# An adaptive-norm transformer layer on one core: the join of attention and MLP, its loads, its projection and its weight splits

## The chip, the cores and the metric

The kernel runs on one core of a Trainium2 chip. The metric is the device time of one execution in microseconds; lower is better. TensorE (PE) multiplies, VectorE (DVE), ScalarE (ACT) and GpSimd (POOL) work on tiles, SyncE (SP) issues most DMAs. Each engine runs its own list of instructions in order and waits on semaphores for the others.

## The reference, cut

```python
mod = (silu(c) @ wmod).reshape(8, 6, 1, 512)
sa, ca, ga, sb, cb, gb = (mod[:, i] for i in range(6))
ga, gb = ((2 * (g >= 0) - 1) * maximum(abs(g), 0.25) for g in (ga, gb))
h = layernorm(x) * (1 + ca) + sa                 # x: 8 x 512 x 512
x = x + ga * attention(h, W_attn, W_proj)        # 16 heads of 32, causal
h = layernorm(x) * (1 + cb) + sb
x = x + gb * (relu(relu(h @ W1.T + b1) @ W2.T + b2) @ W3.T + b3)   # 512-1024-1024-512
```

## The kernel before

Each fp32 product is made of three products of a high and a low part: a `hi` step rounds a tile to the matmul's format on ScalarE, a `lo` step subtracts it from the whole value on VectorE, and TensorE multiplies hi*hi, hi*lo and lo*hi (`TERMS`). A tile of weights therefore needs a `_hi` and a `_lo` step before its first use.

**Attention** runs batch by batch, 0 to 7. A batch has eight slots p (pairs of heads), a slot has five units u. In unit (p, u) TensorE makes scores by query of pair p, scores by key of pair p - 2, in units 1 and 3 the weighted values of pair p - 3 (10 matmuls of each of two kinds), and pieces of the QKV projection. VectorE takes row maxima from the scores (two score banks), splits the maxima into `max_rows` in unit 2, and two DMAs of 4 KB carry them into `stack`, where the key scores of pair p - 1 need them in the next slot. ScalarE exponentiates key scores twice (`prob_hi`, `prob`), GpSimd (four units) and VectorE (one) make `prob_lo`. The last batch goes on to slot 11, with no projections of a next batch; its scores end in slot 7, its key scores in slot 9, its weighted values in slot 10.

**The join.** In the slots of that batch every engine calls a function `early(p, u)` at the end of each unit, which begins the second half of the layer in that engine's list; `rest()` follows when the slots are over. What is to be done for the first batch k = 0 (and partly k = 1): load `at` (attention output), `wproj`, `xt` (`res_tiles`), the gate `ga` and four blocks of W1; turn `at` with transposes (`TURNED`, four times four) through two `aux` banks and split it (`turned_hi`, `turned_lo`); project it, four tiles of 12 matmuls (`PROJ`); gate, add the residual and take statistics (`rows(t)` on VectorE); the inverse deviation on GpSimd; normalise on ScalarE; turn again (`ROWS`), modulate into `h2`. Tiles of this half lie on SBUF that attention has used, so a load waits until its place is free: the methods of `Released` wait on attention's semaphores for that.

**The MLP** is a Strassen-like scheme of seven products per layer and batch: n = 0 to 7 are the chunks of the first layer (`expand`), 8 to 15 of the second, 16 to 23 of the third. Operand s of chunk n is made by sums on VectorE, `hi(n, s)` and `lo(n, s)`; the W1 side needs four sums (`w1_sum`) and seven splits (`w1_hi`, `w1_lo`). Between the products of chunk k stand the aux pieces of later batches (`AUX_AT`): PROJ(k+1, 2) and (k+1, 3) after products 0 and 1, TURNED(k+2) in 2 and 3, ROWS(k+1) in 5 and 6.

The names `w_0` to `w_6` in the lists below are the seven splits of W1 (`w_s_whole` is the whole value), `lin` and `aux` are PSUM banks, `op` is an MLP operand, `gated`, `res_tiles` and `bn_stats` belong to `rows(t)`.

## Time and profile before

| | us |
|---|---|
| median of three runs | 1503.06 (1500.37 to 1503.61) |
| the profiled execution | 1500.26 |
| its span, first to last instruction | 1498.5 |
| PE busy in the span | 1432.5 (96%) |
| DVE busy | 1111.7 (74%) |
| ACT busy | 811.2 (54%) |
| POOL busy | 447.9 (30%) |

### The profile page before, as it was taken

The page shows a single profiled execution, that of the slowest core. Times are in us where ns is not written, and L with a number is a line of the kernel's source. Part 1 is how long each engine was busy: PE and PEld are TensorE (multiplying, and loading weights), DVE is VectorE, ACT ScalarE, POOL GpSimd, SP SyncE. Part 2 cuts the span into 40 slices and gives each one's busy share as a digit, 9 for nine tenths or more (in the row PEclk, how much of TensorE's full clock was granted, in tenths as well). Part 3 has the DMA queues.
Part 4 walks back from the last instruction along what each step waited for, and adds up shares of the span by engine and source line. Part 5 has one row for each costly group of instructions (what it writes and reads, how often), then busy time and mean ns, then how long its engine had stood idle before and what let it go on. Part 6 is the DMA issues. An engine that isn't in the chain of part 4 may idle for free. (4 is left out here: it accounts for less than half of the span.)

```text
span 1498.5 us, 30337 instructions
## 1 busy us (share of the span) xinstructions
PE 1432.5 (96%) x12048; PEld 1284.9 (86%) x12048; DVE 1111.7 (74%) x1955; ACT 811.2 (54%) x1468; POOL 447.9 (30%) x450
## 2 busy tenths in 40 slices
PE   7999999999999999988699999999999999999998
PEld 4578787887878878876599999999999999999998
DVE  4687777777877777668676666797766676788887
ACT  3366666667676767666555555566333333354331
POOL 2375765666576667655200000000000000000000
PEclk9999999999999999999799999999999999999999
DMA  8625354443534343473344444644756556589985
GB/s 275 157 55 128 93 135 94 110 114 78 125 88 122 83 122 82 101 203 116 106 148 148 148 149 148 221 173 150 271 199 218 204 211 235 210 290 311 298 298 181
DMA packets 126589, 247.15 MB, mean 165 GB/s; under 512 B 13672, under 2 KB 36200, under 8 KB 126448
## 3 DMA queue, kind: packets, MB, share of 16 engines
q1 hardware_dynamic: 122416, 241.56, 51.6%
q10 hardware_dynamic: 4032, 3.66, 0.8%
q8 instruction: 95, 1.56, 0.4%
q14 instruction: 46, 0.38, 0.1%
HBM read 114.58 MB, written 79.72 MB: 130 GB/s over the span
## 5 line engine op out<-in xcount | busy, mean ns | idle before, releaser
L537 POOL TENSOR_TENSOR prob_lo<-prob,prob_hi 128x512 f16<-128x512 f32 x256 | 300.6, 1178 | 162.1 <-ACT prob L670 161.7
L663 ACT ACTIVATE prob_hi<-key_score 128x512 f16<-128x512 f32 x320 | 191.1, 597 | 150.8 <-PE key_score L1000 149.3
L2399 PE MATMUL sum_b<-op,w 128*128 128x256 f32 x1728 | 217.9, 284 | 3.4 <-DVE p_c L1957 1.7
L887 PE MATMUL lin<-h_parts,wqkv 128*128 128x512 f32 x768 | 215.1, 403 | 3.7 <-POOL h_parts L497 2.8
L2399 PEld LDWEIGHTS sum_b<-op,w 128*128 128x128 f32 x1728 | 211.3, 192 | 5.7 <-issue 3.7
L845 DVE TENSOR_REDUCE row_max<-score 128x1 f32<-128x512 f32 (+2 forms) x384 | 180.3, 498 | 22.1 <-PE score L987 21.3
L670 ACT ACTIVATE prob<-key_score 128x512 f32<-128x512 f32 x320 | 190.6, 596 | 0.0
L887 PEld LDWEIGHTS lin<-h_parts,wqkv 128*128 128x128 f32 x768 | 139.4, 191 | 33.5 <-DVE h_parts L718 5.4
L987 PE MATMUL score<-stack 96*128 96x512 f32 (+3 forms) x512 | 154.7, 363 | 0.0
L2399 PE MATMUL sum_e<-op,w 128*128 128x256 f32 x1152 | 146.7, 284 | 2.3 <-issue 1.4
L1000 PE MATMUL key_score<-stack 98*128 98x512 f32 (+3 forms) x512 | 143.8, 343 | 4.7 <-DMA stack<-max_rows 4.7
L2399 PE MATMUL sum_a<-op,w 128*128 128x256 f32 x1152 | 145.5, 284 | 0.9 <-issue 0.9
L2399 PEld LDWEIGHTS sum_e<-op,w 128*128 128x128 f32 x1152 | 141.7, 192 | 3.2 <-issue 1.6
L2399 PEld LDWEIGHTS sum_a<-op,w 128*128 128x128 f32 x1152 | 141.2, 192 | 1.8 <-issue 1.0
L1020 PEld LDWEIGHTS o_bank<-v_parts,prob_hi 128*128 128x128 f16 x1280 | 98.4, 98 | 23.5 <-issue 20.8
L1020 PE MATMUL o_bank<-v_parts,prob_hi 128*128 128x97 bf16 x1280 | 115.0, 210 | 0.9 <-issue 0.9
L1020 PE MATMUL o_bank<-v_parts,prob_lo 128*128 128x65 bf16 x1280 | 112.0, 194 | 0.0
L897 PE MATMUL lin<-wqkv,h_parts 128*128 128x256 f32 x768 | 108.8, 284 | 0.0
L897 PEld LDWEIGHTS lin<-wqkv,h_parts 128*128 128x128 f32 x768 | 102.1, 190 | 5.0
L1020 PEld LDWEIGHTS o_bank<-v_parts,prob_lo 128*128 128x128 f16 x1280 | 99.8, 99 | 0.2
L2332 PE MATMUL aux<-wproj,turned 128*128 128x512 f32 x384 | 94.7, 399 | 2.8 <-DVE gated L1824 1.5
L1000 PEld LDWEIGHTS key_score<-stack 98*128 98x128 f32 x512 | 83.9, 193 | 6.1 <-DMA stack<-max_rows 6.0
(164 smaller groups left out, 2555.7 us busy)
## 6 DMA issues: line engine op xcount, KB each, us to landing
stack<-qk_parts SPq DMA_DIRECT2D x384, 128.0 KB, 2.4
late_op_whole<-y_dram SPq DMA_DIRECT2D x40, 512.0 KB, 5.3
y_dram<-u_c SPq DMA_DIRECT2D x32, 512.0 KB, 3.4
blk<-y_dram SPq DMA_DIRECT2D x32, 512.0 KB, 4.2
y_dram<-y_sum SPq DMA_DIRECT2D x24, 512.0 KB, 3.5
x_tiles<-x SPq DMA_DIRECT2D x32, 256.0 KB, 3.7
attn_dram<-o_rows SPq DMA_DIRECT2D x32, 256.0 KB, 2.3
attn_tiles<-attn_dram SPq DMA_DIRECT2D x8, 1024.0 KB, 6.1
```

What stands on the lines that cost most here:

```text
L537: nc.gpsimd.tensor_tensor(prob_lo[:, key[1] % 2, u, :], prob[:, u, :], prob_hi[:, key[1] % 2, u, :], ALU.subtract).then_inc(lo_pool, 1)
L663: nc.scalar.activation(prob_hi[:, q % 2, u, :], bank[:], ACT.Exp, scale=SOFTMAX_SCALE, bias=P_SHIFT)
L670: nc.scalar.activation(prob[:, u, :], bank[:], ACT.Exp, scale=SOFTMAX_SCALE, bias=P_SHIFT)\
L845: last = nc.vector.reduce_max(row_max[:, p % 2, hh, t:t + 1], bank[:, col:col + P * (t + 1)], AX.X)
L887: mm = nc.tensor.matmul(lin_bank_of((QK, f))[:], wqkv[:, wl, c, at:at + P], h[:, hl, c, :], start=(c == 0 and k == 0), stop=(c == NC_ - 1 ...
L897: mm = nc.tensor.matmul(lin_bank_of((V, g, t))[:, 0:C // 2], h[:, hl, c, t * P:(t + 1) * P], wqkv[:, wl, c, at:at + C // 2], start=(c == 0 ...
L987: mm = nc.tensor.matmul(bank[:, col:col + n], rows[:, 0, t * P:(t + 1) * P], rows[:, 1, 0:n], start=False, stop=True, skip_group_check=True)
L1000: mm = nc.tensor.matmul(bank[:, col:col + n], rows[:, 1, t * P:(t + 1) * P], rows[:, 0, t * P:T], start=False, stop=True, skip_group_check ...
L1020: mm = nc.tensor.matmul(o_bank[:, i * VW + low:(i + 1) * VW], part[:, p % 2, u, at:at + P], v[:, j, head, low:VW], start=(j == 0 and part ...
L2332: mm = nc.tensor.matmul(bank[:], turned[:, dl, c, t * P:(t + 1) * P], wproj[:, wl, c, :], start=(c == 0 and i == 0), stop=(c == NC_ - 1 an ...
L2399: mm = nc.tensor.matmul(dst, w[:, wl, c, cols], data[:, dl, c, :], start=begin, stop=end, skip_group_check=again)
```

## The change

- **SBUF.** The QKV weights become two tensors, `wqk` and `wv`; the tensors of the second half are placed in another order, so that `wproj`, `norm_tiles` and `attn_tiles` lie where the query and key weights were. Those weights are last read in unit (3, 1), the value weights in slot 4.
- **SyncE.** The loads for k = 0 and 1 are 256 KB each (W1's too, so `w1_in` counts 32), one a unit, and each unit from slot 3 on first waits for that unit's last score (`unit_reached`). `wproj` is issued at (3, 2) to (4, 0), `at` of batch 0 in slot 4, `xt` in slot 5; before, they were issued at (4, 3) and (5, 0).
- **TensorE.** TURNED of batch 0 moves from slot 6 to units (5, 2) to (6, 0). Its projection, four times 12 matmuls in slots 7 and 8, becomes sixteen times 3, one a unit from (6, 0) and two in (8, 4). The ROWS transposes stand together at (10, 4).
- **ScalarE and VectorE.** The splits of `wproj` and `turned` move with them. `rows(t)` moves to (6, 4), (7, 3), (8, 2), (9, 0); the last sum of W1 to (10, 0), the inverse deviation (GpSimd) to (9, 1). The splits of W1: before, 1 to 6 in a row after operand 0; now split 1 at (10, 4), ahead of operand 0 on VectorE, and 2 to 6 between the steps of the first chunk.
- **ScalarE in every expand chunk:** `hi(n, 6)` ahead of `relu(n, C11)`, not behind it.

```diff
         def early(p, u):
-            if (p, u) == (NEXT_FROM, 3):
+            if p >= 3:
+                released.unit_reached(sp, p, u)
+            if (p, u) == (3, 2):
+                released.query_key_weights(sp)
+            if p == 3 and u >= 2:
+                load_proj(u - 2)
+            if (p, u) == (4, 0):
+                load_proj(3)
+            if p == 4 and u:
+                load_at_tile(0, u - 1)
+            if (p, u) == (5, 0):
                 released.projections(sp)
-                released.projections_taken(sp)
-                load_at(0)
-                sp.dma_start(wproj_whole[:, 1], wproj_t.rearrange("(c p) n -> p c n", p=P)).then_inc(proj_in, 16)
...
+        def unit_reached(self, engine, p, u):
+            if p < PAIRS:
+                engine.wait_ge(score_done, unit_no(B - 1, p, u) + 1)
+            elif p < PAIRS + 2:
+                engine.wait_ge(key_done, unit_no(B - 1, p - 2, u) + 1)
...
         def early(p, u):
-            if p == 6 and u in (1, 2):
-                proj_lo(u - 1)
-            if p == 6 and u:
-                turned_lo(0, u - 1)
-            if p == 7 and u < 2:
-                w1_sum(u)
-            if p in (7, 8) and u in (2, 4):
-                rows(2 * (p - 7) + u // 2 - 1)
+            if (p, u) == (4, 4):
+                proj_lo(0)
+            if (p, u) == (5, 1):
+                proj_lo(1)
+            if p == 5 and u >= 2:
+                turned_lo(0, u - 2)
+            if (p, u) == (6, 0):
+                turned_lo(0, 3)
+            if (p, u) in ((6, 4), (7, 3), (8, 2), (9, 0)):
+                rows(((6, 4), (7, 3), (8, 2), (9, 0)).index((p, u)))
+            if (p, u) == (7, 1):
+                w1_sum(0)
             if (p, u) == (8, 0):
+                w1_sum(1)
+            if (p, u) == (8, 3):
                 w1_sum(2)
-            if (p, u) == (8, 4):
+            if (p, u) == (9, 0):
                 variance(0)
...
+            if (p, u) == (10, 0):
                 w1_sum(3)
...
+            if (p, u) == (10, 4):
+                w1_lo(1)
...
+        def project_part(k, t, c):
+            bank = aux_bank[AUX_NO[(PROJ, k, t)] % 2]
+            if k == 0 and t == 0 and c % 2 == 0:
+                pe.wait_ge(w_ready, W_NO[("proj", c // 2)] + 1)
+            if t == 0:
+                pe.wait_ge(att_lo, NC_ * k + c + 1)
+            if c == 0:
+                aux_free((PROJ, k, t))
...
         def early(p, u):
-            if p == 6 and u < NC_:
-                aux((TURNED, 0, u))
-            if p in (7, 8) and u in (0, 2):
-                aux((PROJ, 0, 2 * (p - 7) + u // 2))
+            if p == 5 and u >= 2:
+                aux((TURNED, 0, u - 2))
+            if (p, u) == (6, 0):
+                aux((TURNED, 0, 3))
+            if p in (6, 7, 8):
+                part = UNITS * (p - 6) + u
+                project_part(0, part // NC_, part % NC_)
+            if (p, u) == (8, 4):
+                project_part(0, 3, 3)
...
+            hi(n, 6)
             relu(n, C11)
-            hi(n, 6)
```

The three `early` functions above are SyncE's, VectorE's and TensorE's; the last three lines are ScalarE's `expand`.

SyncE's list at the end of attention, from the store of a group of output rows on, before:

```order
L447 DMA attn_dram<-o_rows 128x4x128
L1311 DMA attn_tiles<-attn_dram 128x4x512
L1393 DMA wproj_whole<-wproj_t 128x4x512
L1317 DMA res_tiles<-x 128x4x512
L1322 DMA gate_attn<-gate_dram 128x512 x2
L447 DMA attn_dram<-o_rows 128x4x128
L453 DMA stack<-max_rows 1x8x128 x2
L1401 DMA w_0_whole<-w_t 128x2x512
L1402 DMA w_2_whole<-w_t 128x2x512
```

and now:

```order
L464 DMA attn_dram<-o_rows 128x4x128
L1426 DMA wproj_whole<-wproj_t 128x512 x4
L1420 DMA attn_tiles<-attn_dram 128x512 x4
L1423 DMA res_tiles<-x 128x512
L464 DMA attn_dram<-o_rows 128x4x128
L1423 DMA res_tiles<-x 128x512
L470 DMA stack<-max_rows 1x8x128 x2
L1423 DMA res_tiles<-x 128x512 x2
L1349 DMA gate_attn<-gate_dram 128x512
L1433 DMA w_0_whole<-w_t 128x512 x2
L470 DMA stack<-max_rows 1x8x128 x2
```

The loads have become single tiles, `wproj` comes first, and the maxima (`stack<-max_rows`) have tiles of `res_tiles` and W1 between them instead of whole blocks.

TensorE's list around the start of the projection, at units (7, 0) and (7, 1) before:

```order
L969 MATMUL score<-mask_qk,ident_bf 128x128
L974 MATMUL key_score<-mask_kq,ident_bf 128x128
L987 MATMUL score<-stack 128x512
L1000 MATMUL key_score<-stack 128x512
L2332 MATMUL aux<-wproj,turned 128x512 x12
L969 MATMUL score<-mask_qk,ident_bf 128x256
L974 MATMUL key_score<-mask_kq,ident_bf 128x256
L987 MATMUL score<-stack 128x384
L987 MATMUL score<-stack 128x128
L1000 MATMUL key_score<-stack 128x128
L1000 MATMUL key_score<-stack 128x384
```

and at (6, 0) and (6, 1) now (the last transposes of `attn_tiles` ahead of the first quarter):

```order
L1004 MATMUL score<-stack 128x512
L1017 MATMUL key_score<-stack 128x512
L2404 MATMUL aux<-ident,attn_tiles 128x128 x4
L2416 MATMUL aux<-wproj,turned 128x512 x3
L986 MATMUL score<-mask_qk,ident_bf 128x256
L991 MATMUL key_score<-mask_kq,ident_bf 128x256
L1004 MATMUL score<-stack 128x384
L1004 MATMUL score<-stack 128x128
L1017 MATMUL key_score<-stack 128x128
L1017 MATMUL key_score<-stack 128x384
```

Twelve projection matmuls behind one unit have become three behind each, and they begin a slot earlier.

VectorE's list from the last gather of attention to the first gate of the first chunk, before:

```order
L809 TENSOR_REDUCE o_sum<-o_bank 128x4x32
L812 RECIPROCAL o_rcp<-o_bank 128x4
L1859 TENSOR_TENSOR op_sum<-h 128x512
L1917 TENSOR_TENSOR op<-h,op 128x512
L1981 TENSOR_TENSOR w_1<-w_1_whole,w_1 128x1024
L1981 TENSOR_TENSOR w_2<-w_2_whole,w_2 128x1024
L1981 TENSOR_TENSOR w_3<-w_3_whole,w_3 128x1024
L1981 TENSOR_TENSOR w_4<-w_4_whole,w_4 128x1024
L1981 TENSOR_TENSOR w_5<-w_5_whole,w_5 128x1024
L1981 TENSOR_TENSOR w_6<-w_6_whole,w_6 128x1024
L1824 TENSOR_TENSOR gated<-aux,gate_attn 128x512
```

and now:

```order
L826 TENSOR_REDUCE o_sum<-o_bank 128x4x32
L829 RECIPROCAL o_rcp<-o_bank 128x4
L2050 TENSOR_TENSOR w_1<-w_1_whole,w_1 128x1024
L1928 TENSOR_TENSOR op_sum<-h 128x512
L1986 TENSOR_TENSOR op<-h,op 128x512
L1893 TENSOR_TENSOR gated<-aux,gate_attn 128x512
L1934 TENSOR_TENSOR op_whole<-h,op_sum 128x512
L1941 TENSOR_TENSOR op_sum<-op_whole,h 128x512
```

Five of the six splits of W1 are gone from ahead of the gate; split 1 has moved ahead of the first operand's sum and split.

## Rows read from the trace of the kernel before

**Rows 1.** The page's slices, 37.5 us each: TensorE and its granted clock.
```profile
PE   7999999999999999988699999999999999999998
...
PEclk9999999999999999999799999999999999999999
```

**Rows 2.** Windows: us, busy (xcount) of PE, PEld, DVE, ACT, POOL, PEclk, DMA share, GB/s.
```profile
662.40:674.15 11.75, 8.14 (x68) 6.33 (x68) 5.75 (x15) 5.32 (x12) 5.43 (x6) 0.71 0.91 324
674.15:685.45 11.30, 7.62 (x84) 6.27 (x84) 9.80 (x20) 8.39 (x15) 7.47 (x6) 1.00 0.66 230
685.45:700.21 14.76, 13.43 (x94) 10.48 (x92) 10.81 (x21) 5.82 (x11) 5.38 (x5) 0.77 0.25 69
700.21:709.40 9.19, 9.12 (x81) 7.32 (x80) 8.44 (x18) 6.20 (x12) 6.48 (x5) 1.00 0.22 84
709.40:729.47 20.07, 8.04 (x69) 6.55 (x70) 12.27 (x21) 11.10 (x20) 10.44 (x9) 0.67 0.19 66
...
653.85:740.17 86.32, 65.38 (x562) 53.98 (x560) 58.13 (x114) 51.15 (x93) 42.65 (x38) 0.82 0.43 136
665.00:672.00 7.00, 5.49 (x35) 4.30 (x36) 2.65 (x7) 2.56 (x5) 2.84 (x3) 0.51 1.03 374
685.60:692.40 6.80, 5.47 (x15) 3.85 (x13) 4.27 (x6) 2.56 (x5) 3.87 (x3) 0.50 0.22 73
716.30:733.40 17.10, 8.73 (x66) 8.05 (x67) 6.27 (x13) 7.33 (x12) 3.86 (x4) 0.50 0.13 48
```

**Rows 3.** Timeline of TensorE: start, us, what, in brackets the wait ahead and its releaser.
```profile
666.51 0.80 PE L1000 MATMUL key_score<-stack 98*128 98x512 f32 x1 [3.54 <-DMA stack<-max_rows]
...
717.74 1.11 PE L2320 MATMUL aux<-ident,attn_tiles 128*128 128x128 f32 x4 [4.24 <-DVE turned L1814]
...
729.47 0.90 PE L2342 MATMUL aux<-ident,norm_tiles 128*128 128x128 f32 x3 [6.93 <-ACT norm_tiles L1588]
...
740.17 3.03 PE L2399 MATMUL sum_a<-op,w 128*128 128x256 f32 x24
...
744.70 3.06 PE L2332 MATMUL aux<-wproj,turned 128*128 128x512 f32 x12 [1.50 <-DVE gated L1824]
```

**Rows 4.** SyncE's timeline at slot 4's end, then the page's DMA issues (us to landing).
```profile
659.53 0.36 SPq L1311 DMA_DIRECT2D attn_tiles<-attn_dram  x1
...
x_tiles<-x SPq DMA_DIRECT2D x32, 256.0 KB, 3.7
...
attn_tiles<-attn_dram SPq DMA_DIRECT2D x8, 1024.0 KB, 6.1
```

**Rows 5.** VectorE's groups by form, 660 to 745 us, and GpSimd's timeline beside L1991.
```profile
L1814 DVE TENSOR_TENSOR turned<-aux,turned 128x512 fp32r<-128x512 f32 x8 | 5.5, 683 | 5.1 <-ACT turned L1580 5.1
...
L1976 DVE TENSOR_TENSOR wproj<-wproj_whole,wproj 128x1024 fp32r<-128x1024 f32 x2 | 2.7, 1354 | 0.4 <-ACT wproj L1657 0.4
...
L1991 DVE TENSOR_TENSOR w_whole<-w_whole,w_whole 128x1024 f32<-128x1024 f32 x1 | 2.1, 2071 | 0.0
...
L1995 DVE TENSOR_TENSOR w_whole<-w_whole,w_whole 128x1024 f32<-128x1024 f32 x1 | 1.2, 1216 | 0.0
...
688.28 1.16 POOL L537 TENSOR_TENSOR prob_lo<-prob,prob_hi 128x512 f16<-128x512 f32 x1 [0.31 <-ACT prob L670]
```

**Rows 6.** Timeline of VectorE.
```profile
697.63 0.67 DVE L1824 TENSOR_TENSOR gated<-aux,gate_attn 128x512 f32<-128x512 f32 x1
...
700.00 0.72 DVE L845 TENSOR_REDUCE row_max<-score 128x1 f32<-128x384 f32 x2
...
743.96 0.68 DVE L1824 TENSOR_TENSOR gated<-aux,gate_attn 128x512 f32<-128x512 f32 x1
...
761.02 0.68 DVE L1917 TENSOR_TENSOR op<-op_sum,op 128x512 fp32r<-128x512 f32 x1
```

**Rows 7.** Timeline of ScalarE ahead of the ROWS transposes.
```profile
726.49 2.93 ACT L1588 ACTIVATE norm_tiles<-res_tiles,mlp_shift,rstd 128x512 f32<-128x512 f32 x4 [2.35 <-DVE mlp_shift L1850]
```

**Rows 8.** Waits of TensorE from 747 to 1025 us: total, times, longest.
```profile
PE sum_b L2399 <- DVE p_c L1957: 1.7, 7, 0.3
```

More of the change, by code:

```diff
@@ L258, in w_block, with w_part @@
         return tile[:, :, W_ORDER[k]:W_ORDER[k] + W_BLOCK]
+    def w_part(part, k):
+        first = W_ORDER[k]
+        if first < 2 * C:
+            return wqk[:, part, :, first:first + W_BLOCK]
+        return wv[:, part, :, first - 2 * C:first - 2 * C + W_BLOCK]
     def w_ready(f):
@@ L1227, in mlp @@
     const_in, gb_in = mem.sem("const_in"), mem.sem("gb_in")
-    at_in, proj_in = mem.sem("at_in"), mem.sem("proj_in")
+    at_in = mem.sem("at_in")
+    proj_in = [mem.sem(f"proj_in{i}") for i in range(2)]
     w1_in = [mem.sem(f"w1_in{i}") for i in range(4)]
@@ new lines, in early @@
+        def early(p, u):
+            if p >= 3:
[9 more added lines that the diff above has]
+            if (p, u) == (5, 0):
+                released.projections(sp)
+            if p == 5 and u < NT:
+                load_x_tile(0, u)
+            if (p, u) == (5, 4):
@@ L1407, in early @@
-            if (p, u) == (6, 3):
-                load_x(1)
+            if (p, u) == (6, 0):
+                released.value_rest(sp)
+            if p == 6 and u < 4:
+                load_w1(u // 2, u % 2)
+            if (p, u) == (6, 4):
+                released.key_scores(sp, 3)
+            if (p, u) in ((6, 4), (7, 0)):
+                load_w1(2, p - 6)
+            if (p, u) in ((7, 1), (7, 2)):
+                load_w1(3, u - 1)
+            if (p, u) in ((7, 3), (7, 4), (8, 0), (8, 1)):
+                load_at_tile(1, 2 * (p - 7) + (u - 3 if p == 7 else u))
@@ L1653, in proj_hi @@
         def proj_hi(half):
-            if half == 0:
-                act.wait_ge(proj_in, 16)
+            act.wait_ge(proj_in[half], 32)
             c = 2 * half
@@ L1712, in rest @@
             released.probabilities(act)
-            for s in range(1, STEPS):
+            for s in (1, 2):
                 w1_hi(s)
@@ L1730, in expand @@
             first_product(n)
+            if n == 0:
+                w1_hi(3)
             hi(n, 3)
+            if n == 0:
+                w1_hi(4)
             hi(n, 4)
+            if n == 0:
+                w1_hi(5)
+                w1_hi(6)
             if last:
@@ L2127, in rest @@
             lo(0, 0)
-            for s in range(1, STEPS):
-                w1_lo(s)
             released.outputs(dve)
@@ L2156, in expand @@
                 add_rows(k + 1, 1)
+            if n == 0:
+                w1_lo(2)
             lo(n, 2)
+            if n == 0:
+                w1_lo(3)
             if k == B - 2:
@@ L2321, in turn_attention @@
             mm.then_inc(aux_done, 1)
-        def project(k, t):
-            bank = aux_bank[AUX_NO[(PROJ, k, t)] % 2]
-            if k == 0 and t == 0:
-                pe.wait_ge(w_ready, W_NO[("proj", 1)] + 1)
-            if t == 0:
-                pe.wait_ge(att_lo, NC_ * (k + 1))
-            aux_free((PROJ, k, t))
+        def project_part(k, t, c):
+            bank = aux_bank[AUX_NO[(PROJ, k, t)] % 2]
+            if k == 0 and t == 0 and c % 2 == 0:
+                pe.wait_ge(w_ready, W_NO[("proj", c // 2)] + 1)
+            if t == 0:
+                pe.wait_ge(att_lo, NC_ * k + c + 1)
+            if c == 0:
+                aux_free((PROJ, k, t))
+            for i, (wl, dl) in enumerate(TERMS):
+                mm = nc.tensor.matmul(bank[:], turned[:, dl, c, t * P:(t + 1) * P], wproj[:, wl, c, :],
+                                      start=(c == 0 and i == 0), stop=(c == NC_ - 1 and i == 2))
+            if c == NC_ - 1:
+                mm.then_inc(aux_done, 1)
+        def project(k, t):
             for c in range(NC_):
-                for i, (wl, dl) in enumerate(TERMS):
-                    mm = nc.tensor.matmul(bank[:], turned[:, dl, c, t * P:(t + 1) * P], wproj[:, wl, c, :],
-                                          start=(c == 0 and i == 0), stop=(c == NC_ - 1 and i == 2))
-            mm.then_inc(aux_done, 1)
+                project_part(k, t, c)
         def turn_rows(k, c):
@@ L2407, in early @@
         def early(p, u):
-            if p == 6 and u < NC_:
-                aux((TURNED, 0, u))
-            if p in (7, 8) and u in (0, 2):
-                aux((PROJ, 0, 2 * (p - 7) + u // 2))
+            if p == 5 and u >= 2:
+                aux((TURNED, 0, u - 2))
+            if (p, u) == (6, 0):
+                aux((TURNED, 0, 3))
[4 more added lines that the diff above has]
+                project_part(0, 3, 3)
             if p == 9 and u < NC_:
                 aux((TURNED, 1, u))
-            if p == 10 and u < NC_:
-                aux((ROWS, 0, u))
+            if (p, u) == (10, 4):
+                for c in range(NC_):
+                    aux((ROWS, 0, c))
             if p == 11 and u in (1, 3):
```

115 lines of the change are left out of this document (68 added, 47 removed).

## The prediction

> **What bounds the kernel now.** The page comes first: its slices show TensorE at nine tenths or more nearly everywhere except at the start and in slices 18 to 20, and the clock dips in one of those slices too [rows 1]. 37 us a slice puts the place at 640 to 750 us, where attention hands over to the MLP. Second come windows cut at the borders of the attention slots [rows 2]. From 653.85 us (last batch, slot 4) to 740.17 us (first MLP product [rows 3]) there are 86.3 us, of which TensorE is busy 65.4, so 20.9 us are idle. Three stretches stand at half clock (5.5, 5.5 and 8.7 us of busy time), so about half of 19.7 us, 9.8 us, is lost to the clock. At full clock and without a gap TensorE would need 55.6 us. Third comes the timeline of TensorE: it waits 3.54 us for two 4 KB rows of maxima (slot 5), 4.24 us for VectorE's split of turned attention (slot 9), 6.93 us for ScalarE's normalised rows before the ROWS transposes, 1.50 us for VectorE in the first products [rows 3]. The other engines say what would be next: VectorE is busy 58.1 us of the same 86.3 [rows 2], more than TensorE's 55.6 us of true work. Behind the join, TensorE has next to no waits (0.3 us in each of seven expand chunks [rows 8]), so what is gained before the first product reaches the end of the program one for one.
>
> **Slots 5 to 9, the base.** They run 11.75, 11.30, 14.76, 9.19 and 20.07 us, 67.1 us to the ROWS transposes at 729.47; slot 5 carries attention alone, 5.75 us of VectorE [rows 2]. Prices on VectorE: a quarter-megabyte split of wproj 1.35 us, half of turned 0.6 us (0.68 each, overlapped in sequence), sums of W1 2.07 us once and 1.2 us afterwards [rows 5], a group of gate, residual and statistics 697.63 to 700.00, 2.4 us [rows 6].
>
> **Loads one slot sooner.** Before, 3 MB are issued from 659.53 us on and the rows of maxima have to get through them [rows 4]; that is the 3.54 us wait. After it, wproj goes out in four portions behind the stack rows, some 3 us before that time, and the attention tiles one a unit from 658 us. I take 2 MB over some 8 us instead of 3 MB at once, and take the wait from 3.54 to 1 us; bounds 0 and 3.54. What is behind it on SP: the maxima of slots 5 to 8 stand in the same queue, each behind at most the portion of the unit before. Here the Trainium skill ("DMA: Bandwidth & Descriptors", Rules for kernel authors) speaks against the change: for bandwidth it wants 1 MiB or more in a DMA. The trace agrees in part: 256 KB land in 3.7 us and 1024 KB in 6.1 us [rows 4], so four portions one behind another would take 14.8 us where one took 6.1. By that rule the last attention tile, issued at about 662.5, would have to wait for its predecessors and land near 673 rather than 666, and the gain would be about 5 us smaller; the transfers of the profile overlap, so I keep to 3.7 us.
>
> **Slot 5.** VectorE now has 5.75 of attention, both wproj splits (2.7; the first falls at slot 4's end) and three turned splits (1.8): 10.3 us, and I add 1.4 us of hand-overs where it waits for ScalarE's high parts: 11.7 us. The slot is no shorter than before (11.75), but it carries work that before filled slot 6.
>
> **Slots 6 and 7.** TensorE: attention at full clock 5.3 us (slot 7's 14.76 less 1.3 idle, 2.7 clock and two projections of 2.7) and five quarters of 0.69: 8.8, with the last transpose 9.2. VectorE: 5.75 + 0.6 + 2.4 = 8.8 in slot 6; 5.75 + 2.07 + 2.4 = 10.2 in slot 7. The longer one counts: 9.3 and 10.2. Before it was 11.30 + 14.76.
>
> **Slot 8.** Keys alone. VectorE: gathers, maxima and one low part 2.3, two sums of W1 2.4, one group of rows 2.4: 7.1; TensorE six quarters 4.1 and attention 3.4: 7.5. With one hand-over (the turn of the maxima waits for slot 7's last maximum) 8.0.
>
> **Slot 9 up to ROWS.** The last group of rows 2.4, variance 0.2, four turned splits in step with TensorE and ScalarE, then the last probabilities of the pair, the normalisation 2.9 [rows 7]: 12.5 us. Before 20.07: there W1's fourth sum and first split stood ahead of the turned splits and the deviation stood behind the last low parts on GpSimd; after, it is asked for at (9, 1) and lies ready, and the sum and the split (1.2 + 1.2 to 2.2) lie in the shadow of ScalarE. The normalisation itself stays exposed.
>
> These five give 11.7 + 9.3 + 10.2 + 8.0 + 12.5 = 51.7 us against 67.1: **15.4 us** gained.
>
> **ROWS to the first product.** Before 740.17 - 729.47 = 10.7 us, four of them at half clock. After: four transposes paced by ScalarE's modulation 2.8 us, two projections of 2.8: 8.4 us, **2.3 us** gained. VectorE has a new wait here: W1's split 1 stands ahead of the first operand and needs ScalarE's copy, which stands behind modulation and the operand's copy. I put the operand at 7.6 us from the first ROWS transpose, so 0.8 us before TensorE wants it: it costs nothing; without that cover it would be up to 1.2 us.
>
> **First products.** Before, six splits in a row held up the gate of VectorE until 743.96, and TensorE waited 1.50 us [rows 3, 6]. After, that gate stands ahead of four of them: 1.5 us gained. Given back: five splits, 5.8 us, now stand between the sums of the first chunk. From 743.96 to the split of operand 5 at 761.02 VectorE does not pause [rows 6], 17.7 us with that split. It starts 0.8 us before the first product and so ends 17.7 + 5.8 - 0.8, or 22.7 us, behind it; TensorE wants operand 5 at 21.9. I charge 0.8 us, bounds 0 and 3. Net **0.7 us**.
>
> **Order on ScalarE in every expand chunk.** Copy 6 goes ahead of four relus. Before, the sum of C22 stood behind it and TensorE waited 0.3 us in seven chunks, 1.7 us in all [rows 8]. I take all of it: **1.8 us** with the first chunk. The relus move back by 0.5 us and nobody waits for them so closely.
>
> Of the other edits (split of the QKV tensor in two, places of tiles, 32 in place of 16 to wait for) nothing takes time of its own. The number of matmuls and of bytes stays.
>
> **Sum.** 15.4 + 2.3 + 0.7 + 1.8 = 20.2 us. Against it I set what such a sum doesn't see: TensorE still idles some 4 us of 12 in slots 5 and 9, and each of the two shorter dips of before began after idle time and cost 2.7 us. I take one (2.7) and 1.5 us for hand-overs between the engines: 4.2. The gain is **16 us**. The profiled execution took 1500.26 us (span 1498.5 and 1.8 around it), so 1484.3. The three runs have a median of 1503.06 and reach from 1500.37 to 1503.61, so the profiled one is at their lower end; I put the forecast at **1485**.
>
> Port of VectorE and GpSimd: the first sum of W1 takes 2.07 us with GpSimd at work beside it from 688.28 on, and the others 1.2 us [rows 5]. The Trainium skill ("SBUF — State Buffer", Who interferes with whom) says that a VectorE instruction with two SBUF inputs contends with a GpSimd instruction that reads SBUF. Both splits of wproj and a second and a third sum of W1 now lie in slots in which GpSimd works most. By that rule all of them could cost 2.1 rather than 1.2 to 1.35 us, and the gain would be up to 3 us smaller.
>
> **Rivals.**
> 1. VectorE is the wall. It has 45 us of work in slots 5 to 9 and I let it be busy 88% where it was busy 70% (47.1 of 67.1 [rows 2]). If it stays at 78%, the five slots take 58 us, 6 us more, and two dips instead of one cost 2.7: 1494. For: the pieces come in threes behind ScalarE's copies, and TensorE has only two banks of scores. Against: in slot 8 before, it was busy 8.44 of 9.19.
> 2. Nearly everything goes: no dip and no hand-overs beyond those in the slots, 1500.3 - 20.2 = 1480, and if slot 5 is not bound by VectorE 3 to 5 us less, 1476. For: slots with projection in them had no gaps before (slot 8, 9.12 of 9.19).
> 3. Slower: the maxima wait behind portions. The place is the first key score of slots 5 to 9. If the 4 KB rows meet a portion in flight in each and wait the measured 3.54 us, and each wait brings a dip of 2.7 us, it is five times 6.2, 31 us, less the one such wait and dip of before (6.2): 25 against the gain of 20.2, 1505. It turns at about 80% of that price in every slot. Against: the DMA engines were 0.91 busy over the whole of slot 5 [rows 2], and only that one wait came of it.
> 4. It doesn't do what it says: the portions come too late for (5, 2), each unit holding the next load back, and the order gains nothing in slots 5 and 6; the later parts stay: about 1497 to 1500.
>
> **How the numbers follow.** Forecast 0.55, rival 1 0.22, rival 2 0.13, rival 3 0.05, rival 4 0.05. The range 1476 to 1495 holds the first three with their bounds (nine in ten, and some lies beyond). A measurement here tells 0.2%, 3 us, from no change. Faster takes the first three and a part of rival 4, 0.92; same the rest of rival 4, 0.03; slower 0.05.
>
> **What would show it.** The wait of TensorE for the maxima at the first key score of slot 5 at 1 us or less; turned splits in slot 5; the first batch's projection in threes, nowhere twelve in a row; ROWS at about 714 and the first product at 722 to 725; no 1.5 us wait at the second projection of the first chunk, a wait of up to 1 us at operand 5; no wait at C22. Half clock in 10 us or less of the join instead of 31. Wrong, if VectorE's share in slots 5 to 9 is below 80% while TensorE waits for it, or if TensorE waits for maxima in more than one slot.

## The result and the profile after

The changed kernel took 1490.26 us (median of four runs, 1489.35 to 1492.82) beside 1502.53 us for the kernel before; ratio **0.9914, 95% interval 0.9897 to 0.9931**. Two later comparisons gave 0.9901 (0.9880 to 0.9922) and 0.9897 (0.9878 to 0.9916). The gain is 12 to 15 us; 1485 was forecast.

The profiled execution took 1489.35 us, span 1487.6, that is 10.9 us less than the span before. The page's slices of TensorE and its granted clock [rows 1 before]:

```profile
PE   8999999999999999999799999999999999999998
PEclk9999999999999999999999999999999999999999
```

The slices at 8, 8 and 6 in the middle have become 9, 9 and 7, and the clock's 7 is gone. Windows cut at the same borders as in [rows 2] (slots 5 to 9, the ROWS transposes up to the first product, the whole from slot 4 to the first product, and the two stretches of half clock in it):

```profile
667.99:677.78 9.79, 8.40 (x80) 7.20 (x81) 8.65 (x18) 8.34 (x16) 6.97 (x6) 0.83 0.68 216
677.78:688.42 10.64, 9.84 (x88) 7.34 (x86) 8.48 (x21) 6.65 (x14) 5.62 (x6) 1.00 0.60 176
688.42:697.62 9.20, 9.17 (x83) 6.86 (x83) 8.92 (x18) 5.41 (x12) 6.67 (x5) 1.00 0.51 147
697.62:706.34 8.72, 8.05 (x74) 5.88 (x74) 7.34 (x15) 6.74 (x13) 5.88 (x6) 1.00 0.47 150
706.34:722.51 16.17, 8.73 (x111) 7.46 (x110) 13.65 (x24) 10.08 (x18) 9.65 (x8) 0.86 0.45 147
722.51:731.73 9.22, 8.90 (x43) 7.10 (x41) 4.09 (x7) 5.49 (x7) 0.62 (x1) 0.88 0.72 235
659.44:731.73 72.29, 61.41 (x561) 49.20 (x560) 56.59 (x114) 49.40 (x90) 41.89 (x38) 0.93 0.60 182
670.00:673.00 3.00, 3.00 (x20) 2.40 (x21) 2.37 (x5) 2.78 (x6) 2.35 (x3) 0.52 0.96 343
717.80:725.20 7.40, 5.56 (x52) 4.79 (x52) 3.94 (x6) 3.15 (x5) 2.27 (x3) 0.54 0.19 70
```

From slot 4 to the first product it is 72.3 us in place of 86.3: TensorE idles 10.9 us and not 20.9, and two stretches at half clock, some 10 us, are left of 31. VectorE was busy 56.6 of the 72.3 us.

But the span shrank by 10.9 us only, while the join gave 14.0 and the part behind it 2.4. The rest went the other way **ahead** of the join: slot 4 of the last batch starts at 659.44 in place of 653.85 us, 5.6 us later, in a part whose order of work the change leaves alone. The timeline of TensorE, with the waits that are left:

```profile
669.98 0.69 PE L1017 MATMUL key_score<-stack 98*128 98x512 f32 x1 [1.39 <-DMA stack<-max_rows]
...
709.25 0.20 PE L1037 MATMUL o_bank<-v_parts,prob_hi 128*128 128x97 bf16 x1 [1.57 <-DVE o_rcp L829]
...
712.52 0.66 PE L2404 MATMUL aux<-ident,attn_tiles 128*128 128x128 f32 x4 [1.56 <-DVE turned L1883]
...
718.00 0.24 PE L1037 MATMUL o_bank<-v_parts,prob_hi 128*128 128x97 bf16 x1 [2.60 <-POOL prob_lo L554]
...
721.15 0.27 PE L1037 MATMUL o_bank<-v_parts,prob_hi 128*128 128x97 bf16 x1 [1.63 <-DVE o_rcp L829]
...
722.51 3.47 PE L2431 MATMUL aux<-ident,norm_tiles 128*128 128x128 f32 x16
...
731.73 3.04 PE L2488 MATMUL sum_a<-op,w 128*128 128x256 f32 x24
734.61 2.91 PE L2416 MATMUL aux<-wproj,turned 128*128 128x512 f32 x12
...
754.14 1.67 PE L2488 MATMUL sum_e<-op,w 128*128 128x256 f32 x12 [0.64 <-DVE w L2050]
```

Against [rows 3]: the wait for the maxima went from 3.54 to 1.39 us and that for the split of turned attention from 4.24 to 1.56; the 6.93 us are gone, and so is the 1.50 us at the second projection (734.61 carries no wait). New between slot 9's start and ROWS are 2.60 us for GpSimd's low part and 1.57 and 1.63 us for VectorE's gatherings, and behind the first product 0.64 us at operand 5. SyncE's timeline, to set beside [rows 4]:

```profile
662.68 0.54 SPq L464 DMA_DIRECT2D attn_dram<-o_rows  x1
663.33 3.07 SPq L1426 DMA_DIRECT2D wproj_whole<-wproj_t  x4
666.51 2.15 SPq L1420 DMA_DIRECT2D attn_tiles<-attn_dram  x4
668.76 0.38 SPq L1423 DMA_DIRECT2D res_tiles<-x  x1
```

The portions did not go out one a unit: they left back to back. What SyncE did ahead of them, and the longest of its waits from 650 to 669 us (total, times, longest):

```profile
654.68 7.90 SPq L428 DMA_DIRECT2D stack<-qk_parts  x12
```

```profile
SPq L411 <- DVE qk_parts L739: 4.0, 1, 4.0
```

SyncE waited 4.0 us for VectorE's `qk_parts`, then issued attention's twelve transfers of them, 0.64 us each, and only then reached the store of `o_rows` and the portions behind it in its order. Counted from slot 4's start, `wproj` went out at 3.9 us, before at 6.1; the attention tile was issued at 7.1 to 9.2 us, and before at 5.7 us (659.53 against 653.85): **not sooner at all**. Its four portions took 4.7 us to landing (median), the last of them 5.6, so that the tile was whole at 673.9 us.

The maxima that TensorE waits for in slot 5 do not pass through SyncE. ScalarE issues them (the last ones before that wait):

```profile
665.57 0.65 ACTq L695 DMA_DIRECT2D stack<-max_rows  x1
...
666.25 0.63 ACTq L695 DMA_DIRECT2D stack<-max_rows  x1
```

From slot 6 on they are SyncE's.

### The profile page after: what moved, and what is told of

It reads as the page before. It is cut to its first block and busy times, and to the rows that moved or that the text cites. A ratio compares the mean times of both kernels' runs of the same rounds, so it can differ in the third digit from the quotient of the medians.

```text
span 1487.6 us, 30364 instructions
## 1 busy us (share of the span) xinstructions
PE 1434.5 (96%) x12048; PEld 1286.3 (86%) x12048; DVE 1107.9 (74%) x1955; ACT 811.3 (55%) x1468; POOL 447.3 (30%) x450
## 3 DMA queue, kind: packets, MB, share of 16 engines
q8 instruction: 95, 1.56, 0.4%
## 5 line engine op out<-in xcount | busy, mean ns | idle before, releaser
L904 PE MATMUL lin<-h_parts,wqk 128*128 128x512 f32 x768 | 215.9, 404 | 3.5 <-POOL h_parts L514 2.8
L904 PEld LDWEIGHTS lin<-h_parts,wqk 128*128 128x128 f32 x768 | 140.8, 192 | 32.4 <-DVE h_parts L735 4.4
L914 PE MATMUL lin<-wv,h_parts 128*128 128x256 f32 x768 | 108.8, 284 | 0.0
L914 PEld LDWEIGHTS lin<-wv,h_parts 128*128 128x128 f32 x768 | 102.1, 190 | 5.0
L986 PE MATMUL score<-mask_qk,ident_bf 128*128 128x256 bf16 (+1 forms) x320 | 82.9, 259 | 7.1 <-DVE row_max L858 6.8
```

Source lines behind the costliest of these rows:

```text
L904: mm = nc.tensor.matmul(lin_bank_of((QK, f))[:], wqk[:, wl, c, at:at + P], h[:, hl, c, :], start=(c == 0 and k == 0), stop=(c == NC_ - 1 a ...
L914: mm = nc.tensor.matmul(lin_bank_of((V, g, t))[:, 0:C // 2], h[:, hl, c, t * P:(t + 1) * P], wv[:, wl, c, at:at + C // 2], start=(c == 0 a ...
```

## The experiments

All variants are edits of the changed kernel. Their medians lie within 5 us of each other, hardly more than one interval (3 to 4.5 us to either side), so their verdicts rest on three stretches of the profiles, cut at TensorE's turns of the maxima (matmuls named turn). J is the stretch from the turn of slot 4 (2.88 us behind the slot's start) to the first product, E from there to the span's end, S the last of J's pieces, from the last turn (2.3 us into slot 8) to the first product.

| kernel | turn of slot 4 at | J | S | E | median us | ratio to before (95%) |
|---|---|---|---|---|---|---|
| before, three profiles | 656.7, 662.0, 661.7 | 83.4, 82.0, 81.7 | 36.5, 36.3, 36.4 | 758.3, 758.3, 758.5 | 1502.53, 1503.94, 1503.87 | |
| changed, three profiles | 662.3, 659.6, 661.6 | 69.4, 69.6, 69.4 | 31.8, 32.1, 31.9 | 755.9, 755.9, 757.0 | 1490.26, 1488.72, 1488.67 | 0.9897 (0.9878 to 0.9916), the last |
| behind_gather | 663.8 | 68.9 | 31.3 | 756.6 | 1488.64 | 0.9897 (0.9874 to 0.9920) |
| both_moves | 658.0 | 70.0 | 30.0 | 756.7 | 1488.87 | 0.9901 (0.9880 to 0.9921) |
| rows_late | 660.2 | 67.1 | 29.3 | 755.7 | 1487.26 | 0.9892 (0.9873 to 0.9912) |
| whole_loads | 658.7 | 72.4 | 32.0 | 756.3 | 1492.17 | 0.9918 (0.9893 to 0.9943) |
| half_loads | 658.1 | 71.3 | 32.2 | 756.6 | 1490.40 | 0.9919 (0.9898 to 0.9940) |
| whole_tiles | 661.1 | 72.7 | 35.1 | 755.9 | 1492.09 | 0.9918 (0.9889 to 0.9946) |
| splits_in_row | 658.7 | 71.7 | 32.3 | 756.4 | 1488.13 | 0.9889 (0.9860 to 0.9918) |
| relu_first | 661.4 | 69.3 | 31.9 | 757.4 | 1488.76 | 0.9897 (0.9872 to 0.9921) |

**Is the later attention a price of the change?** Both kernels again, with no edit.

> The kernel before once more, unchanged, for a second profile of its attention part. Theory (chance): the 5.6 us by which the attention part of the changed kernel runs later up to its fourth slot (start of the join) is three stretches of half clock at batch boundaries and a clock that rises later at the start, and a single execution has them or not; another profile of the kernel before may have them too, and the join from the fourth slot's start to the first product stays at 86 us, within 1. Rival (placement): the other places of the attention weights in the changed kernel make its attention slower; then this profile has no such stretch, as the first one.

> The changed kernel once more, unchanged. Time 0.991 of the kernel before by both theories. Chance: the fourth slot starts anywhere from 654 to 660 us, with none to three stretches of half clock at the batch boundaries, and the join from there to the first product stays at 72.3 us, within 1. Placement: the fourth slot starts at 659 to 660 us again, with the same three stretches.

Windows of one batch's length, all around the same batch boundary: from the kernel before's first profile, from r_before, from r_after (columns as above):

```profile
414.95:495.79 80.84, 78.17 (x745) 65.49 (x744) 62.67 (x146) 54.83 (x109) 52.63 (x53) 1.00 0.44 108
```

```profile
419.36:501.70 82.34, 79.59 (x746) 67.09 (x745) 61.91 (x146) 54.80 (x109) 52.74 (x53) 0.98 0.43 106
```

```profile
416.32:497.84 81.52, 78.20 (x745) 65.48 (x744) 62.69 (x146) 54.86 (x109) 52.70 (x53) 1.00 0.43 107
```

The same instructions (745 and 746 matmul records) take 78.2 us of TensorE at clock 1.00 or 79.6 at 0.98. The changed kernel has this too: in its first profile the batches of 335.14 to 417.81 and 417.81 to 500.00 us took 79.6 at 0.98. The third window, at full clock, is still 0.7 us longer than the first, as TensorE waits 1.2 us for a row maximum in it. The first profile of the kernel before had no such stretch in seven; its second had four, the first of the changed kernel three, its second two. Chance holds: the kernel before reaches the fourth slot at 656.7 and 662.0 us, the changed one at 659.6. The 5.6 us were a comparison with one lucky execution. What was expected of the join missed: J of r_before is 82.0 us, 1.4 less than in the first profile. A third profile of each:

> The kernel before a third time, unchanged, to judge the attention part. So far its two profiles reach the turn of the fourth slot of the last batch at 656.7 and 662.0 us, and the eleven profiles of the changed kernel and its variants at 658.0 to 663.8; the last stretch of one batch up to there takes 79.4 us in both of before, and 80.8 in seven of the eleven, 79.4 to 79.7 in four. Theory (chance): anywhere from 656 to 664, the last stretch 79.4 or 80.8. Rival (placement makes attention slower in the changed kernel): below 660 and 79.4. From the turn of the fourth slot to the first product 81.5 to 84 us, from there to the end 758.3 within 0.7, by both.

> The changed kernel a third time, beside the two others of this call. Time 1487 to 1491 us, from the fourth slot's turn to the first product 69.5 us within 1, from there to the end 755.9 within 0.5; the fourth slot starts anywhere from 654 to 661 us, by the number of half-clock stretches at the batch boundaries.

661.7 and 661.6 us. J of before was 81.7, so the first profile, with a join of 83.4, was the longest of three there: by the means J fell by 12.9 us, from 82.4 to 69.5.

One thing stays open: the stretch from slot 4's turn in batch 6 to that in batch 7 (the boundary stretch below) took 79.4 us in all three profiles of before, and 80.8 to 80.9 in the three of the changed kernel (and in four of its eight variants; 79.4 to 79.7 in the other four). The longer ones have a stretch of half clock at the last batch boundary: the granted clock is 0.88 from 578 to 592 us in the changed kernel's first profile, and 1.00 at the same place of before (575 to 589). If it is a price, it is 1.4 us; three against three doesn't settle it, and the four variants without it speak for chance.

E of 757.0 in r_after2 missed what was expected (755.9 within 0.5). That profile has a stretch of half clock in the MLP, from 1331.6 to 1335.0 us, where the first one has full clock; and whole_loads and half_loads, which edit nothing behind the first product, come to 756.3 and 756.6. So differences of E under 1 us are not read from one profile below.

**Size of the portions.**

```diff
-            if p == 3 and u >= 2:
-                load_proj(u - 2)
...
+            if (p, u) == (4, 2):
+                released.batch_output(sp, 0)
+                sp.dma_start(at[:], rows_of(attn_dram, 0)).then_inc(at_in, 16)
...
-            if p == 5 and u < NT:
-                load_x_tile(0, u)
+            if (p, u) == (5, 0):
+                load_x(0)
```

This is whole_loads; half_loads cuts the same loads into 512 KB. The whole `wproj` and `at` go out a unit or two later in the program than their first portions, at (4, 0) and (4, 2).

> The changed kernel with the projection's weights, the first batch's attention tile and its residual tile each loaded by one transfer of 1 MB, at the units where their first portion went out. Theory (queue): a transfer of 1 MB in flight holds the small transfer of the maxima, for which TensorE waited 3.5 us in the fifth slot before; the wait of 1.4 and 0.7 us in the changed kernel grows to 3 us or more in one of the slots 4 to 6, a stretch of half clock follows, and the join from the turn of the fourth slot to the first product takes 72 to 75 us instead of 69.5. Rival (the Trainium skill, DMA: Bandwidth & Descriptors, rules for kernel authors, large transfers are cheaper): the whole loads land sooner, nothing waits longer, 69.5 or less. The size alone makes no difference: 69 to 70.

> The changed kernel with the same four loads (projection weights, attention tile, residual tile of the first batch) in portions of 512 KB in place of 256 KB. Theory (queue): TensorE's wait for the maxima in the fifth slot goes by the size in flight ahead of them: 0.8 and 1.4 us with 256 KB portions, 3.8 with 1 MB, so about 2 us here (1.5 to 2.8), and the stretch from the fourth slot's turn to the next takes 10 to 11.5 us (9.0 and 9.7 with 256 KB, 12.2 with 1 MB). Rival (it goes by the total of bytes in flight, not by the portion): the wait is as with 256 KB, 1.4 or less. Second rival (by the time at which SyncE issues, not by size): the wait is 3 or more, as with 1 MB, since all are issued within 5 us in every version.

TensorE's first key score of slot 5, with 1 MB, with 512 KB, with 256 KB portions (the changed kernel's third profile), and with 256 KB in both_moves, a variant further down:

```profile
668.79 0.80 PE L1017 MATMUL key_score<-stack 98*128 98x512 f32 x1 [3.84 <-DMA stack<-max_rows]
```

```profile
667.28 0.50 PE L1017 MATMUL key_score<-stack 98*128 98x512 f32 x1 [2.98 <-DMA stack<-max_rows]
```

```profile
669.18 0.65 PE L1017 MATMUL key_score<-stack 98*128 98x512 f32 x1 [1.36 <-DMA stack<-max_rows]
```

```profile
667.06 0.80 PE L1017 MATMUL key_score<-stack 98*128 98x512 f32 x1 [2.81 <-DMA stack<-max_rows]
```

In the nine profiles with 256 KB the wait is 0.57 to 1.60 us eight times, seven of them with a second one of 0.3 to 0.8 in slot 6, and 2.81 us in both_moves, whose edits lie slots later. So 1 MB stands apart with 3.84 us; 512 KB, with 2.98 where about 2 was expected, does not. Nor is it shown that the portion is what counts. Of the loads that SyncE had issued and that had not landed when ScalarE issued the second row of maxima there were 0.5 MB (wait 0.57 us, splits_in_row), 0.75 MB (0.61 to 1.36, five profiles), 1 MB (1.39, 1.60, 2.81), 1.5 MB (2.98, half_loads), 2 MB (3.84, whole_loads) and 3 MB (3.54 to 3.81, the kernel before). The bytes in flight order the waits as well as the portions do, and no run holds one of them fixed.

J is 2.9 and 1.9 us longer, but not by the portions alone. Both runs had the short boundary stretch, and the slots behind a short one were longer with 256 KB too. From slot 4's turn to the last turn:

| portions | boundary stretch 80.8 to 80.9 | boundary stretch 79.4 to 79.7 |
|---|---|---|
| 256 KB | 37.3 to 37.8 (seven profiles) | 40.1 (both_moves), 39.5 (splits_in_row) |
| 512 KB | | 39.2 |
| 1 MB | | 40.4 |

Counted with the boundary stretch, from slot 4's turn in batch 6 to the first product, the loss against the changed kernel's three profiles is 1.5 us with 1 MB (151.8 against 150.3) and 0.7 with 512 KB. Against the two 256 KB runs with a short boundary stretch 1 MB loses 0.3 and 0.9 us up to the last turn, and 512 KB nothing. The size of the portions is worth at most 1.5 us of the gain, and perhaps nothing. The rule of the Trainium skill (DMA: Bandwidth & Descriptors, Rules for kernel authors: 1 MiB or more for bandwidth) is about bandwidth; what TensorE waits for here is a 4 KB transfer beside the large ones.

**Projection in quarters.**

```diff
-            if p in (6, 7, 8):
-                part = UNITS * (p - 6) + u
-                project_part(0, part // NC_, part % NC_)
-            if (p, u) == (8, 4):
-                project_part(0, 3, 3)
+            if (p, u) in ((6, 3), (7, 2), (8, 1), (8, 4)):
+                aux((PROJ, 0, ((6, 3), (7, 2), (8, 1), (8, 4)).index((p, u))))
```

> The changed kernel with the first batch's projection in four blocks of twelve matmuls (3 us each) in place of sixteen quarters. Theory (filling): a quarter of 0.8 us fits into the wait of each unit, a block of 3 us delays the next unit's scores and with them VectorE, so slots 6 to 8 together (the turns 60 to 63 from slot 4) take 2 to 4 us more than 28.5, and the first product comes 1.5 to 4 us later than 69.5 behind the fourth slot's turn. Rival (VectorE is the limit in these slots): TensorE catches up in the units without a block; under 1 us.

J is 3.3 us longer, as expected, but not where it was expected: the turns of slots 5 to 8 span 28.8 us, where the changed kernel's took 27.9 to 28.5 and 30.5 or more was expected. The loss lies in S, 35.1 in place of 32. TensorE there, then VectorE:

```profile
698.70 0.27 PE L1070 MATMUL turn<-ident,row_max 128*8 128x128 f32 x1 [0.77 <-POOL prob_lo L554]
...
699.62 4.52 PE L2416 MATMUL aux<-wproj,turned 128*128 128x512 f32 x12
...
705.65 0.69 DVE L868 TENSOR_TENSOR prob_lo<-prob,prob_hi 128x512 f16<-128x512 f32 x1 [4.83 <-ACT prob L687]
```

A block at half clock behind two waits takes 4.5 us, ScalarE gets no key scores meanwhile, and VectorE stands 4.83 us. Quarters are worth 3.3 us in this one profile, the largest single share of the join that a run isolates.

**Splits of W1 between the first products.** All six once more in a row, on ScalarE and VectorE (the lines `w1_lo(2)` to `w1_lo(6)` and `w1_hi(3)` to `w1_hi(6)` leave expand):

```diff
             lo(0, 0)
+            for s in range(1, STEPS):
+                w1_lo(s)
             released.outputs(dve)
```

> The changed kernel with the splits of W1's blocks 1 to 6 once more in a row behind operand 0, as before. From the first product to the end the two profiles of before took 758.3 and 758.3 us, the two of the changed kernel 755.9 and 755.9. Theory (the sum of the prediction): of these 2.4 us the splits between the first products are worth 0.7, and this run takes 756.3 to 757.0. Rival: they are worth nothing, since the operands' wait only moves from the second to the sixth product; 755.9 within 0.2. Second rival: they carry all of it; 758.3. The join ahead of the first product stays within 1 us of 69.5 (from the turn that opens the fourth slot), as nothing ahead of it is touched.

```profile
726.95 6.90 DVE L2043 TENSOR_TENSOR w<-w_whole,w 128x1024 fp32r<-128x1024 f32 x6 [0.26 <-ACT w L1724]
733.77 0.68 DVE L1886 TENSOR_TENSOR gated<-aux,gate_attn 128x512 f32<-128x512 f32 x1
...
734.51 3.04 PE L2400 MATMUL aux<-wproj,turned 128*128 128x512 f32 x12 [1.09 <-DVE gated L1886]
```

The wait at the second projection is back, that at operand 5 is gone. A group of sum_e products in the second chunk that starts 59.01 us behind the first product in r_after (59.01 to 59.07 in the three profiles) starts 59.58 us behind it here: 0.57 us. E is 756.4. J was 2.2 us longer, a miss; nothing edited lies in it ahead of S, its slot 6 ran at clock 0.77 (10.32 us busy), and the boundary stretch was the short one (79.44); counted with it 0.8 us remain.

**Order on ScalarE.**

```diff
-            hi(n, 6)
             relu(n, C11)
+            hi(n, 6)
```

> The changed kernel with the high part of operand 6 once more behind the ScalarE relu, as before, in both halves of each batch. Theory (the sum): this is the 1.8 us of the prediction, seven waits of 0.3 us; from the first product to the end it takes 757.4 to 758.0 us in place of 755.9, and the waits for the combination of products are there seven times again. Rival: the wait is covered by the next matmuls and only moves, 756.2 or less.

Waits of TensorE over the whole span (total, times, longest):

```profile
PE sum_b L2488 <- DVE p_c L2026: 1.8, 6, 0.5
```

In the changed kernel's three profiles 0.3 us or less is left of this row. E is 757.4, 1.5 us above the two profiles of the changed kernel without half clock in the MLP. The waits come back, so the mechanism is right; the size, some 1.5 us by the waits and by E, is a little under the 1.8 taken (E alone could not tell it, see above).

**What sets the last slot.** The first edit moves VectorE's steps; the second also spreads the rows over the units; the third spreads them one unit later, behind the first weighted values:

```diff
-            if (p, u) == (9, 4):
-                w1_lo(0)
-            if (p, u) == (10, 0):
+            if (p, u) == (10, 2):
                 w1_sum(3)
             if (p, u) == (10, 4):
+                w1_lo(0)
```

> The changed kernel with the last sum of W1's blocks and the first low part of W1 taken from in front of the last gathering of row sums on VectorE to behind it. Theory (queue): the last slot ahead of the turned rows took 16.2 us where 12.5 was forecast, since 3.7 us of VectorE's work on W1 stand in front of the gathering for which TensorE waits 1.6 us; the wait goes, the slot gets 1.5 to 3 us shorter, and the time 1 to 3 us (ratio to the changed kernel 0.998 to 0.999). Rival (GpSimd): the low parts of the probabilities on GpSimd end as late as before, TensorE's 2.6 us for them stay, and nothing is gained (under 0.5 us). Second rival: the two steps now end later than the first product wants them, and the first product moves back by what the slot gained, 0 in all.

```diff
-            if (p, u) == (10, 4):
-                for c in range(NC_):
-                    aux((ROWS, 0, c))
+            if p == 10 and u < NC_:
+                aux((ROWS, 0, u))
```

> As the run with the two steps of W1 behind the gathering, and the turned rows once more one in each unit in place of all four behind the weighted values. Theory (queue): the normalised rows are there 3 us before the last slot ends, so the turned rows' 2.9 us fill the waits of TensorE in it; 1 to 3 us less than with the first move alone. Rival: a turned row's bank is taken by VectorE or ScalarE behind other work there, so that the next row waits, and the gain is under 0.5 us.

```diff
+            if p == 10 and u:
+                aux((ROWS, 0, u - 1))
```

> The changed kernel with W1's last sum and first low part behind the last gathering (as in the run with that move alone) and the four turned rows one in each of the units 1 to 4 of the last slot, so that the first stands behind the first weighted values and not ahead of them. From the turn of the last slot to the first product the changed kernel took 31.8 and 32.1 us, the first move alone 31.3, both moves 30.0 with a wait of 4.1 us for the normalised rows. Theory (order): the weighted values fill 1.2 us of that 4.1, so 28.5 to 29.2 us, and the first product still waits for no operand. Rival (ScalarE): ScalarE turns a row's bank over one at a time while a row waits for its bank, 30 us or more. In all 1 to 3 us below the changed kernel, ratio to the kernel before 0.988 to 0.990.

TensorE in rows_late, then in both_moves:

```profile
716.08 0.24 PE L1037 MATMUL o_bank<-v_parts,prob_hi 128*128 128x97 bf16 x1 [2.60 <-POOL prob_lo L554]
...
717.59 1.97 PE L2430 MATMUL aux<-ident,norm_tiles 128*128 128x128 f32 x8
```

```profile
717.60 1.11 PE L2430 MATMUL aux<-ident,norm_tiles 128*128 128x128 f32 x4 [4.12 <-ACT norm_tiles L1647]
```

S is 31.3, 30.0 and 29.3 us against 31.9. Moving VectorE's steps gave only 0.6 us (1.5 to 3 expected): the wait for the gathering shrank from 1.6 to 0.7, and the 2.60 us for GpSimd's low part stayed, as its rival says. The larger part is the second edit's, 1.3 us, and 0.7 more where the weighted values fill the wait for the normalised rows (28.5 to 29.2 was expected of S). A part of these is clock: the granted clock over S is 0.94 in both_moves and rows_late and 0.89 in behind_gather and the changed kernel. So three things together make up the slot: GpSimd's low part, VectorE's queue ahead of the gathering, ROWS behind both value blocks. In both_moves J is 1.1 us longer than in behind_gather all the same, with the wait of 2.81 us in slot 5 and the short boundary stretch. rows_late has the shortest join of all (J 67.1), 2.4 us below the changed kernel; its median, 1.4 us lower on the same chip, can't be told from it by time.

## The prediction, point by point

- **What bounds it: right.** The gain came from the join; 11.5 us (from slot 4's turn in batch 6 to the first product 161.8 before, 150.3 after, means of three), 2.1 us behind it, 0.4 ahead of it: 14.0 in all, where 16 were forecast. The spans' means are 1500.9 and 1486.9. Of the join's share the runs isolate 3.3 us (quarters) and at most 1.5 (portions); that the rest comes of the new order on TensorE, VectorE and GpSimd is read from the profiles and not shown by a run.
- **Slots 5 to 9: 12.6 us where 15.4 were summed** (54.5 in place of 51.7). Slot 5 came out 1.9 shorter, 6 longer by 1.3, 7 shorter by 1.0, 8 longer by 0.7. The mis-sized term is **slot 9 up to ROWS, 12.5 taken, 16.2 measured**. The step that failed reads "the sum and the split ... lie in the shadow of ScalarE": they stood ahead of VectorE's gathering (0.6 us in behind_gather). And the step left out that ROWS follow both blocks of weighted values, of which the first waits 2.60 us for GpSimd (rows_late took another 2.0 us off by placing ROWS between them). The exposed end is these, not the normalisation: norm_tiles were ready at 719.5 and ROWS began at 722.51.
- **Loads one slot sooner: the issue time was wrong, the wait nearly right, its cause half known.** `wproj` went out 1.8 us before the time at which the old loads began, not some 3, and the attention tiles from 7.1 us behind slot 4's start, where the forecast had 4.2 (658), as SyncE was issuing its twelve transfers. The wait fell to 1.39 us, 0.76 and 1.36 in the other two profiles (1 taken). With 1 MB at about the same place it is 3.84, so smaller portions or fewer bytes in flight did this, not an earlier time. "The maxima ... stand in the same queue" holds from slot 6 on; those of slot 5 are ScalarE's. The landing of 3.7 us "kept to" was 4.7 for these four: the last was there 14.4 us behind slot 4's start, between the forecast's 12.2 and the 19.2 of the other rule. TensorE's first turned transpose still came 6.2 us earlier in its slots (14.8 against 20.9 us behind slot 4's start), since it is asked for a slot earlier. Before, the tile landed 9 us before TensorE turned it; after, 0.3 us before (in two of the variants TensorE waited 0.4 and 0.6 us for it). So it seems to be the order of the work that made the join shorter, and the load was only just in time for it. A run with the old order and the new loads was not made.
- **"TensorE waits for maxima in more than one slot" was named as a sign against the forecast.** It does, in slots 5 and 6, 1.39 and 0.70 us; the sign was too sharp, as these cost little. Rival 3 was that mechanism at full price in five slots; it showed at 0.4 and 0.2 of the price in two.
- **ROWS to the first product: 1.5 us where 2.3 were taken**; the stretch's clock was 0.88. VectorE's new wait for ScalarE's copy is there (4.91 us idle ahead of w1_lo(1)), and the operand was ready 1.0 us before TensorE wanted it, 0.8 foretold: it cost nothing.
- **First products: 0.57 us** by splits_in_row, 0.7 taken; the new wait at operand 5 is 0.64 us, 0.8 taken. **Order on ScalarE: some 1.5 us**, 1.8 taken.
- **The allowance of 4.2 us was about right for a partly different reason.** Slots and ROWS gave 14.1 us of 17.7, so 3.6 were missing; slot 9's excess of 3.7 us is as large as that. The 67.1 us are read from the first profile of before, whose join was 1.4 to 1.8 us longer than in the two later ones; from one of those the same sum would have given 14.2 to 14.6 us, and 14.0 were measured between the means. One dip at slot 5 and one at the last slot are left.
- **Rival 1 (VectorE is the wall)**: VectorE was busy 47.0 of 54.5 us, 86% where 88% was foretold and 78% would have been the rival. Only slot 7 is near it (8.92 of 9.20); the others are at 80 to 88%. **Rival 2** needs no dip; three profiles have two each. **Rival 4** came true in its first half (the loads are late) without its price.
- **First product at 722 to 725: 731.73**, but 5.6 us of the difference lie ahead of slot 4. The forecast was set against 1500.3 us, the quickest execution of before that was known then, and had no term for what a single execution catches in 650 us of attention, which is more than any term of the sum but the first.
- **The contention of VectorE and GpSimd, up to 3 us:** the four sums took 1.66, 1.21, 1.53 and 1.63 us, the wproj splits 1.23 and 1.35, the first split 2.11. Against the prices taken the sums cost 0.4 us more and the wproj splits 0.1 less; the first split lies at the upper end of its 1.2 to 2.2.

## To carry to other kernels

A small transfer that an engine waits for is delayed by the large ones in flight beside it, from another engine's queue too: with 2 to 3 MB issued ahead TensorE waited 3.5 to 3.8 us for two rows of 4 KB, with 0.5 to 0.75 MB 0.6 to 1.4. Whether the portion or the total counts is open here, so vary both. When a load is moved up in program order, look in the trace for what its queue is doing at that place, waits and issues alike; the order alone says nothing of its issue time. Cut filler work on TensorE into small pieces, and compare stretches between the same two instructions over several executions before a few us ahead of the edit are explained.

## What the runs showed of the hardware

**Of VectorE and GpSimd the one that begins first keeps its length, the other takes longer.** VectorE and GpSimd in the changed kernel, then in behind_gather:

```profile
716.87 2.11 DVE L2050 TENSOR_TENSOR w<-w_whole,w 128x1024 fp32r<-128x1024 f32 x1
...
716.74 1.16 POOL L554 TENSOR_TENSOR prob_lo<-prob,prob_hi 128x512 f16<-128x512 f32 x1 [0.72 <-ACT prob L687]
```

```profile
723.88 1.20 DVE L2050 TENSOR_TENSOR w<-w_whole,w 128x1024 fp32r<-128x1024 f32 x1
...
724.04 1.51 POOL L565 TENSOR_TENSOR o_rows<-o_sum,o_rcp 128x256 f32<-128x256 f32 x1 [4.11 <-DVE o_rcp L829]
```

GpSimd began first at 716.74 and VectorE's split took 0.9 us more; VectorE began first at 723.88, kept its 1.20, and GpSimd's product took 1.51 us where 0.62 is the median of its 64 (spans of GpSimd are rough in the profile). The Trainium skill ("SBUF — State Buffer", Who interferes with whom) says that issue order decides who blocks; both traces agree.

**The same wait of TensorE at a batch boundary is followed by half clock in some executions and not in others**, with the same matmuls ahead of it. It waits 1.5 to 2.6 us for VectorE's `h_parts`, mostly 1.7: 1.72 us before 421.4 in the first profile of before, 1.73 before 425.9 in r_before, where half clock follows. Each costs 1.4 us of TensorE's time: none, four and four of them in seven boundaries in three profiles of one kernel. What decides it was not tried.
